# Feed-forward and second attention of a two-layer decoder put into one program, with the attention's first products among the feed-forward's last ones

## The reference

```python
x = x + _L0_xattn_ref(_layernorm(x), mask, ctx, ctx, wq, wk, wv, wo)
x = x + _L0_ffn_ref(_layernorm(x), gate_w, gate_b, val_w, val_b, out_w, out_b)      # ternary weights, 8-bit rows
x = x + _L1_xattn_ref(_layernorm(x), ctx, mask, Wq, bq, Wk, bk, Wv, bv, Wo, qn_w, kn_w)
x = x + _L1_ffn_ref(_layernorm(x), router_w, gate_w, up_w, down_w, s_gate_w, ...)   # 8 experts, top 2, and a shared one

# the first feed-forward
gate = silu(bit_linear(x, gate_w, gate_b)); val = bit_linear(x, val_w, val_b)
return bit_linear(gate * val, out_w, out_b)                                         # 512 -> 2048 -> 512

# the second attention: 16 heads of 128 on 4 key heads; q and k are RMS-normalised
q = (hidden_states @ Wq + bq).reshape(b, s, NH, HD).transpose(0, 2, 1, 3)
scores = jnp.einsum('bhsd,bhed->bhse', rmsnorm(q, qn_w), rmsnorm(k, kn_w)) * scale + attention_mask
out = jnp.einsum('bhse,bhed->bhsd', softmax(scores), v)
return out.transpose(0, 2, 1, 3).reshape(b, s, NH * HD) @ Wo
```

## Time and profile before

| | us |
|---|---|
| median of 3 runs (1899.67 to 1900.98) | 1899.9 |
| the profiled execution: its time | 1900.31 |
| the profiled execution: its span, first to last instruction | 1898.6 |
| TensorE busy | 1756.0 (92%) |
| VectorE busy | 1238.1 (65%) |
| ScalarE busy | 852.2 (45%) |
| GpSimd busy | 560.1 (30%) |

### The profile page before, as it was taken

One profiled execution on the slowest core, in us unless ns is written; L12 is line 12 of the kernel. 1 busy time (PEld: TensorE's weight loads), 2 busy tenths in 40 slices (PEclk: granted clock), 3 DMA queues, 4 the chain that ended last, 5 costly groups with the idle time before them and its releaser, 6 DMA issues. The chain is left out here.

```text
span 1898.6 us, 26992 instructions
## 1 busy us (share of the span) xinstructions
PE 1756.0 (92%) x9951; PEld 1448.1 (76%) x9970; DVE 1238.1 (65%) x2357; ACT 852.2 (45%) x1621; POOL 560.1 (30%) x408
## 2 busy tenths in 40 slices
PE   6999996884799948999999999999888999999999
PEld 6989985672344428888888888888766789999876
DVE  4444434776898837766777766778756567676645
ACT  3322321774455525445555544555432255565411
POOL 2111111231666622121321212121120145464342
PEclk9999998997899978999999999999989999999999
DMA  6110114453133364121321212220042378888573
GB/s 221 34 33 22 33 44 145 159 201 117 33 67 79 89 189 136 56 79 57 123 83 62 78 56 79 64 98 6 1 170 112 108 258 274 285 283 267 195 245 106
DMA packets 160945, 225.38 MB, mean 119 GB/s; under 512 B 41654, under 2 KB 101302, under 8 KB 158646
## 3 DMA queue, kind: packets, MB, share of 16 engines
q1 hardware_dynamic: 150940, 189.50, 30.6%
q0 software_dynamic: 9888, 34.35, 5.8%
HBM read 171.65 MB, written 43.78 MB: 113 GB/s over the span
## 5 line engine op out<-in xcount | busy, mean ns | idle before, releaser
L1358 POOL TENSOR_TENSOR a_rq<-a_ssq,a_mhalf 128x4 f32<-128x4 f32 x64 | 65.2, 1018 | 414.5 <-DVE a_ssq L1482 414.5
L78 PE MATMUL bank<-a_xT_hi,a_wq_lo 128*128 128x512 f32 (+1 forms) x384 | 144.2, 375 | 18.8 <-PEq L56 15.8
L1443 ACT ACTIVATE a_pT_hi<-bank 128x512 fp32r<-128x512 f32 x128 | 69.6, 598 | 192.7 <-PE bank L1608 192.6
L1437 ACT ACTIVATE a_scores<-a_scores,a_nmax 128x256 f32<-128x256 f32 x256 | 127.2, 503 | 27.9 <-DVE a_nmax L1497 27.6
L79 PE MATMUL bank<-a_xT_lo,a_wq_hi 128*128 128x512 f32 (+1 forms) x384 | 138.7, 361 | 0.0
L80 PE MATMUL bank<-a_xT_hi,a_wq_hi 128*128 128x512 f32 (+1 forms) x384 | 138.5, 361 | 0.0
L78 PE MATMUL bank<-a_wo_hi,a_oT_lo 128*128 128x512 f32 x320 | 128.3, 401 | 2.8 <-DVE a_oT_lo L416 1.5
L80 PE MATMUL bank<-a_wo_hi,a_oT_hi 128*128 128x512 f32 x320 | 126.7, 396 | 0.0
L79 PE MATMUL bank<-a_wo_lo,a_oT_hi 128*128 128x512 f32 x320 | 126.5, 395 | 0.0
L1490 DVE SCALAR_TENSOR_TENSOR a_scores<-bank,a_rq,a_mask 128x256 f32<-128x256 f32 x256 | 106.1, 477 | 28.7 <-PE bank L80 20.4
L1897 POOL TENSOR_TENSOR e_wg_lo<-raw_g,e_wg_hi 128x1408 fp32r<-128x1408 f32 x26 | 91.4, 3514 | 112.9 <-ACT e_wg_hi L1964 112.9
(11 more groups left out here) (404 smaller groups left out, 5344.1 us busy)
## 6 DMA issues: line engine op xcount, KB each, us to landing
raw_g<-in_egw SPq DMA_DIRECT2D x26, 704.0 KB, 8.6
raw_u<-in_euw SPq DMA_DIRECT2D x26, 704.0 KB, 10.5
a_xT_hi<-x1T_hi SPq DMA_DIRECT2D x16, 1024.0 KB, 6.0
a_xT_lo<-x1T_lo SPq DMA_DIRECT2D x16, 1024.0 KB, 8.2
raw_d<-in_edw SPq DMA_DIRECT2D x26, 512.0 KB, 4.0
y_routed<-m_y SPq DMA_DIRECT2D x39, 256.0 KB
raw_d<-in_edw SPq DMA_DIRECT2D x26, 192.0 KB, 4.3
a_cTraw<-in_ctxT SPq DMA_DIRECT2D x8, 512.0 KB, 3.5
```

Source lines behind the costliest of these rows:

```text
L78: pe.matmul(out, w[1], x[0], start=first, stop=False)
L1358: pool.tensor_tensor(rq[:, h % HG, :], ssq[:, h % HG, :], mhalf[:], ALU.pow).then_inc(s_rq, 1)
L1437: act.activation(row, row, ACT.Exp, bias=nmax[:, i % 2, t:t + 1], accum_out=den[:, i % 2, t:t + 1]).then_inc(s_exp, 1)
L1443: act.activation(pT[b].hi[:], ptb[b][:].rearrange("p (k s) -> p k s", k=QT), ACT.Copy).then_inc(ft.hi, 1)
```

## The change

`ffn0` and `attention1` become one function, `ffn0_attention1`, with one `Phase` and one `Block`. The barrier between them goes. What orders the two parts now is semaphores.

- SBUF: the buffers are placed at fixed offsets in one region. The attention's large buffers lie over those of the feed-forward (scores over the value bias, queries and squares over the normalised rows, output over the hidden rows, the output weight over `x1T`, `x1n` and `hq`); small ones lie behind, some over the place of the next phase's weights.
- PSUM: the next norm's transposes move from bank 4 to 5, the down product from 7 to 6, the feed-forward's transposes from 6 to 7.
- TensorE: queries 0 and 1, sums 0 and 1, scores 0 and 1 and queries 2 stand between the last down products and the transposes of tiles 12 to 15. ACT's, DVE's and POOL's lists follow the same order.
- SP: chunk 0 is loaded as soon as the last up product is done, ahead of tile 15's transpose; chunk 1 and the second keys and values ahead of the stores of tiles 12 to 15. The next phase's weights come behind these stores.
- POOL loads the attention's output weight behind its last work on tile 12.
- New waits: queries 0 for chunk 0, sums 0 for the last copy out of bank 7, scores 0 for the last value bias, the first transposes for the low half of tile 15, the first output for the last addition, and ACT's copy of the output weight for all stores.

The diff, cut to its core (`sp`, `pool`, `act`, `dve` and `pe` are the engines' lists):

```diff
-def ffn0(nc, banks, X, eps, ident, W, gamma, gb6, mv, rstd, b_dram, x1T_dram, ahead, first, wq_dram, ...):
+def ffn0_attention1(nc, banks, X, eps, ident, ones, area, limit, W, gamma, gb6, mv, rstd, b_dram, x1T_dram, ...):
...
+        mem, over = Region(nc, area), Region(nc, area)
+        bv = mem.take("f0_bv", [P, H])
+        xn = mem.take("f0_xn", [P, XS, D])
...
+        sc = [over.take(f"a1_scores{j}", [P, CT, S]) for j in range(2)]
+        q = [over.pair(f"a1_q{j}", [P, C]) for j in range(2)]
...
-        gb, vb = banks[0:2], banks[2:4]
-        x1b = banks[4]
-        xb, ob = banks[6][:].bitcast(BF16), banks[7]
+        gb, vb, x1b, fob, xb = banks[0:2], banks[2:4], banks[5], banks[6], banks[7][:].bitcast(BF16)
+        qb, scb, ptb, ob, ssb = banks[0:2], banks[2:4], banks[4:6], banks[6], banks[7]
...
+            for t in range(T):
+                if t == T - 1:
+                    sp.wait_ge(s_v, T * NH)
+                    for j in range(2):
+                        sp.wait_ge(s_x1st[j], CT // 2 * 32)
+                    chunk(0)
+                hidden_transposed(t)
+                if t >= 4:
+                    next_stored(t - 4)
+            for j in range(2):
+                sp.wait_ge(s_x1st[j], CT * 32)
+            chunk(1)
+            sp.wait_ge(s_flo, len(first.splits))
+            keys_values(1)
+            for t in range(T - 4, T):
+                next_stored(t)
...
+            pool.wait_ge(s_flo, len(first.splits))
+            pool.dma_start(wraw[:], wo_dram[:, 0:HG, :]).then_inc(s_wload, 16)
+            for t in range(T - 3, T):
+                next_rstd(t)
+            rstd(0, 0)
...
             def wo_hi(g):
                 act.wait_ge(s_wload, g * 32 + 16)
+                for s in s_x1st if g == 0 else ():
+                    act.wait_ge(s, T // 2 * 32)
...
+            round_h(T - 1)
+            next_hi(T - 5)
+            next_norm(T - 4)
+            queries(0, 0, 0, True)
+            next_hi(T - 4)
+            next_norm(T - 3)
+            queries(1, 0, 1, True)
+            next_hi(T - 3)
+            exp(0, 0)
+            next_norm(T - 2)
+            queries(2, 0, 2)
+            next_hi(T - 2)
+            next_norm(T - 1)
+            next_hi(T - 1)
...
             def queries(u, begin=False):
...
-                if not begin:
+                if begin:
+                    pe.wait_ge(s_gs, T * NH - 1 + u)
+                    pe.wait_ge(s_chunk[0], 32)
+                    pe.wait_ge(s_flo, len(first.splits))
+                else:
                     pe.wait_ge(fq.lo, u - 1)
+                if n == 1 and h == 0:
+                    pe.wait_ge(s_chunk[1], 32)
...
+            next_xT(T - 5)
+            down(T - 2)
             queries(0, True)
+            next_xT(T - 4)
             queries(1, True)
+            down(T - 1)
             square_sums(0, 0)
+            next_xT(T - 3)
             scores(0)
             queries(2)
             square_sums(1, 1)
+            next_xT(T - 2)
             scores(1)
+            next_xT(T - 1)
```

More of the change, by code:

```diff
@@ L861, in _, with ffn0_attention1 @@
             transposed(T - 1)
-def ffn0(nc, banks, X, eps, ident, W, gamma, gb6, mv, rstd, b_dram, x1T_dram, ahead, first, wq_dram, mask_dram, bq_dram,
-         k_dram, v_dram, T):
+def ffn0_attention1(nc, banks, X, eps, ident, ones, area, limit, W, gamma, gb6, mv, rstd, b_dram, x1T_dram, ahead, first, wq1,
+                    wq_dram, wo_dram, mask_dram, bq_dram, k_dram, v_dram, last, last_drams, B, S, G):
+    T = B * S // P
     H = W[0].shape[2]
@@ L1036, in _, with output @@
+            def output(u, n, i):
+                act.wait_ge(fo.mm, u + 1)
+                if i % HG == 0:
+                    after(act, s_out, n * CT)
+                act.activation(oT.hi[:, i % HG, :], ob[:], ACT.Copy).then_inc(fo.hi, 1)
             act.wait_ge(s_id, 6)
@@ L1040, in _ @@
             xT_copy(1)
[L1041 to L1044 removed]
+            for n in range(T):
+                silu(n, 0)
+                if n >= 1:
                     round_h(n - 1)
[L1046 to L1047 removed]
+                silu(n, 1)
                 if n >= 5:
@@ L1061, in _ @@
                     for pair, raw in first.splits:
-                        act.activation(pair.hi[:], raw, ACT.Copy).then_inc(s_wqhi, 1)
+                        act.activation(pair.hi[:], raw, ACT.Copy).then_inc(s_fhi, 1)
                     act.activation(first.bqg[:], first.bq[:, 0:first.bqg.shape[1]], ACT.Copy)
+            round_h(T - 1)
[12 more added lines that the diff above has]
+            next_hi(T - 1)
+            for u in range(G * U):
+                g, i, n = u // U, u % U, u // HG
+                transposed(u)
+                if u + 1 < G * U:
+                    exp(u + 1, i + 1)
+                if u + 3 < G * U:
+                    queries(u + 3, (u + 3) // U, i + 3)
+                if i == 0:
+                    wo_hi(g)
+                if i == U // 2 and g + 1 < G:
+                    wq_hi(g + 1)
+                if n + 1 < G * NC:
+                    if i % HG == 0:
+                        keys_hi(n + 1)
+                    if i % HG == 1:
+                        values_hi(n + 1)
+                output(u, n, i)
         @block.vector
```

651 lines of the change are left out of this document (304 added, 347 removed).

## The result

| | before | after |
|---|---|---|
| median of 4 runs, us | 1900.2 (1899.7 to 1901.0) | 1874.9 (1872.1 to 1877.1) |
| profiled execution: span, us | 1898.6 | 1872.9 |

The account below looks back on a forecast made before the run. TensorE runs the second attention without a gap, so an earlier start ends the program equally earlier. Start 26.8 us earlier, less 5.8 of tail, gives 21.0: 1900.3 to 1879.3, median 0.4 lower, 1878.9 us; range 1873 to 1887.

Parts of the forecast that it names:

- The chunk: First x1T loads (2 MB), ahead of tile 15's transpose: second issue at 670.0, landing at 680.0, bounds 678.2 and 683.3.
- The term 4.2: First query products of the second attention: 4.2 us with the clock taken as down at their start, bounds 2.8 and 5.6.
- Everything from queries(0) to T0: Attention's start-up with the feed-forward's tail in it: 27.2 us instead of 21.4, from 680.0 to 707.2.
- T0: First transposes of probabilities in the second attention, the mark ending its start-up: at 728.24 before, forecast at 707.2.
- Tile 15's transpose: Queued behind the chunk on SP: issued at 675.85, needed at 687.6, with 7 us of cover.
- The term 21.0: Gain at T0 in us: attention starts 26.8 earlier, less 5.8 of the old tail now in its start-up.
- The clock behind T0: The 9.1 us from T0 on: mean clock 0.70 as before, correction 0, bounds -2.7 and 0.
- Rival D: Gain given back by a new wait: ACT's output-weight copy waits for the last stores; 1899, chance 0.03.
- rival B: Chunk or tile 15's transpose late: 1882.2 to 1884, or 1887 with low clock throughout; chance 0.14.
- rival C: Clock stays up: queries(0) takes 2.8, T0 and queries(3) run full; gain 25.1, 1874.8; chance 0.13.
- Rival E: Slower: buffers' new addresses and banks lengthen the attention's 64 units; 0.4 us more in each makes 1904; chance 0.04.
- the term of 0 for the loop: Attention's loop behind T0: same products in the same order as before, so no gain or loss counted there.

Follow-up runs that it names:

- the first trace: Profile of the merged kernel's first set of runs, the change as described against the kernel before: median 1874.9 us, ratio 0.9866.
- the second trace: Profile of the merged kernel run again with nothing changed, on the same chip as a reordered one: median 1872.5 us, ratio 0.9856 to the kernel before.

## Why the prediction was right, and where it was not

- *The chunk* was said to be issued at 670.0 and to land at 680.0; it was issued at 669.97 and landed at 681.1, inside the bounds. The pair's own time was put at 8.2 us and measures 8.7 where Wo's load isn't beside it; Wo's share was put at 1.8 (2.1 by the second estimate) and measures 2.4. The reason given for taking less than the whole 2.6, that the pair is more than half through when the weight comes, did not fit its own numbers: 2.7 of 8.2 us had passed.
- *queries(0)*, 4.2 us: 5.2 in the first trace (at 1.2 GHz throughout, for which 5.6 was said) and 2.9 in the second. The term 4.2, a clock that rises on the way, came in neither. The clock behind a gap of 3.5 to 3.7 us was at either level here; that could not be forecast from one trace of before.
- *Everything from queries(0) to T0*: T0 was said to be 27.2 us behind the chunk. It is 28.0, of which 1.0 are queries(0). So the chain over POOL, ACT and DVE, with the norms inside the softmax, was right to 0.3 us. It is so step by step and not only in the sum: from the start of the sums of squares the first factor of POOL was ready after 3.8 us (said 3.5) and T0 came after 16.1 (said 16.0; 16.4 in the second trace).
- *Tile 15's transpose* took 5.00 us of SP and still cost nothing: it landed 7.1 us behind its issue, at 683.5, and was needed at 689.7. In the second trace, with queries(0) at full clock, some 3 us of the cover were left.
- *The term 21.0* for T0 measures 19.6 in one trace and 21.8 in the other.
- *The clock behind T0*: 0.75 against 0.70 before, correction -0.4 (-1.0 in the second trace); as said, within -2.7 and 0.
- *Rival D* is refuted by the copy at 716.33, 7.1 us behind T0 (7.6 before). Of *rival B* the low clock throughout queries(0) came true in the first trace, of *rival C* the full clock in queries(0) in the second; the late chunk of B and the full clock at T0 of C did not.
- *Rival E*, and with it the term of 0 for the loop, is the step that failed. The mechanism is real, new addresses change the loop, but its sign was the other one: -3.5 us and not +21. The argument against it, that one operation takes the same time in either of its two buffers, looked at two buffers alike against 64; the prediction did not read the buffers' addresses. This is most of the distance from 1878.9 to 1874.9. That the rest is so small is partly luck: in the profiled execution T0 gained 1.4 us less than said, and the 2.7 us of chance behind unit 60 covered that.
- *The stretch behind the loop*, taken as unchanged, varies from 535.9 to 539.0 us over these kernels, and by 2.9 of these 3.1 us in one and the same program.

The Trainium skill ("TensorE: Matmul & The Clock Gate", section "HAM oscillation — how this bites in real kernels") says that such bursts fall back to the lower clock; scores(1) stand at 702.5 to 704.6 us here, and the clock around them was:

```profile
702.00:704.00 2.00, 1.95 (x15) 1.95 (x16) 0.82 (x3) 1.63 (x3) 0.00 (x0) 0.86 0.66 197
704.00:712.00 8.00, 6.00 (x26) 5.45 (x26) 6.30 (x17) 2.85 (x5) 2.02 (x2) 0.50 0.44 131
```

By that, the trace agrees in part: the clock fell during scores(1), and what follows up to T0 ran at 1.2 GHz, but queries(0), behind the longest wait of all, kept the full clock in the second trace.

## What to carry to other kernels

A border between two phases is worth more by what can be put into its waits than by the barrier: here 8 us for the common program and the early load, 12 to 14 for the interleaving. Whatever is moved ahead in a DMA queue is to be looked at with its neighbours, since the load that nobody waits for takes time from the one that TensorE waits for. When a merge moves buffers, compare where the two operands of the commonest product start before the gain is put down to the order.

## What the runs showed of the hardware

- A product with 512 columns of fp32r takes 227.6 or 233.0 to 233.3 ns by where its operands start in SBUF: moving one by 32 bytes is 3.5 us of the loop. For this projection oT on a multiple of 64 and wo 32 beyond were slow, both on a multiple (227.6) or both 32 beyond (229.2) fast; wo on a multiple with oT 32 beyond was not run. Products of 256 columns whose operands moved by 64 bytes or a little more changed by -1.5 to +1.2 ns, those of the queries, moved by 32, by -1.3. What the rule is stays open.
- The same program had the clock at 1.00 in a burst behind a gap of 3.53 us in one execution and at 0.50 behind one of 3.68 us in another.
- A load of 1 MB on POOL's queue, issued 3.1 us behind a pair of loads of 2 MB on SP's queue, put the pair's landing off by 2.4 us (11.1 and 8.7 us from the second issue).
- A transposing DMA's issue held SP's queue 5.0 to 5.7 us with 2 MB of loads ahead of it and 1 MB on POOL's queue (six traces), 2.0 to 2.5 with either alone (three traces), and 1.5 to 1.6 for the tiles before in the merged kernel, with no such load in flight.
